# Float32 projections in a macaron block: Q, K, V and output products as one full-precision matmul each in place of three split ones

## Chip, cores and metric

The kernel runs on one core of a Trainium2 chip. The metric is the device time of one execution in microseconds (us). A page of the hardware profiler of one execution and the times of three runs are given.

## The reference, cut to what matters

Two batches of 2048 rows of 512 float32 numbers go through three residual steps: half a gated feed-forward block with 4-bit weights, then causal attention with 16 heads of 32, then the same feed-forward block again.

```python
x = L0_attn_X                                   # (2, 2048, 512) float32
x = x + 0.5 * ffn(layernorm(x))
x = x + attn(layernorm(x))
x = x + 0.5 * ffn(layernorm(x))

def attn(X):
    Xn = layernorm(X) * ln_g + ln_b
    Q, K, V = (split_heads(Xn @ W + b) for W, b in ((Wq, bq), (Wk, bk), (Wv, bv)))
    scores = Q @ K.T / sqrt(32)                  # causal mask, softmax, all float32
    AV = softmax(scores) @ V
    return AV @ Wo + bo
```

The change concerns the four products with `Wq`, `Wk`, `Wv` and `Wo`, each (4096 x 512) by (512 x 512), in float32.

## The kernel before, in words

**Order.** Five programs, one for each engine, walk the same plans and meet at semaphores: `tensor_program` (PE), `vector_program` (DVE), `scalar_program` (ACT), `gpsimd_program` (POOL), `sync_program` (SP, which issues all DMAs). Each runs the first feed-forward phase (`ffn_*`, f[0]), then for each batch b the projections (`qkv_*`), the attention (`att_*`) and the output projection (`out_*`), then the second feed-forward phase (f[1]). An engine takes its instructions strictly in the order written.

**Full-precision products out of split ones.** The array multiplies `float32r` operands at reduced precision in one pass. So a float32 operand x is kept as two float32r tiles: hi = x rounded (a copy by ACT or DVE), lo = x - hi (a subtraction by DVE). A product is then three matmuls into one PSUM bank: hi*hi, hi*lo, lo*hi. In this text a "product" is one 128-row by 128-column stationary tile against 128 x 512 moving numbers, and a "bank" is a sum of four products (KC = 4), thus 12 matmuls before.

**Projections** (`Qkv`, lines 828 to 1053). A row block tt holds 512 rows; a batch has four. `Qkv.order` (from line 866) writes the order of a batch: for tt = 0 the four `turn` events (transposes of the twice normed rows) with three `split` events among them, one for each weight matrix; then for each tt eight `features` banks (Q and K, transposed) and four `values` banks, each `values` followed by a `turn` of the next block. The last four `values` banks of a batch are spread over the start of the attention as 16 `value_part` events. A `turn` is four PE transposes into bank 0 or 1, one ACT `activation` with gain and bias into `xnt` (two small buffers, so it waits on `xl_made` of two turns before), then on DVE a copy to `xh` and a subtraction to `xl` (lines 990 to 1013). A `split` is an ACT copy of 128 x 2048 and a DVE subtraction of the same size. `qkv_project` (line 900) issues the three matmuls of each c and waits on `xl_made`. The layernorms of block tt+1 are 48 small DVE instructions, seven after each `features` bank; PE waits for them at the `turn`. The weights Wk and Wq are loaded at the "ahead" event of the last feed-forward block, Wv only after the last store of that phase (`ffn_sp`).

**Attention** (`Att`, lines 1056 to 1438). 160 steps a batch, in four head groups hg, each with query blocks qt = 0 to 3. Scores are f16 matmuls, ACT takes the exponential of each, and `weigh` and `total` are matmuls in true float32 whose stationary tile has 32 columns, four of them side by side in the array (128*32 in the profile). `max` units (96*128 matmuls and a DVE reduction) run ahead at a fixed pace. Into this order the plan puts four `wo_split` events from step (hg, qt, kt) = (2, 3, 0) and four `av_split` events from step (3, 2, 2): each is an ACT copy and a DVE subtraction of 128 x 512, for Wo and for the first quarter of the attention's result `avn`.

**Output projection** (`Out`, lines 1441 to 1580). 16 banks of four products. `out_act` and `out_dve` split the other three quarters of `avn` while PE works; DVE adds each bank to the residual, and does the norms of the next stage beside it. `out_sp` loads the residual rows, then the next weights: for b = 1 the pieces of the second feed-forward phase, of which those that lie where the output weights and split tiles are come late (four gate-and-up pieces, i = 4 to 7, after bank 15).

All matmuls are recorded at line 94 (`Eng.matmul`), transposes at 97, ACT at 100, DVE and POOL two-operand operations at 103, DMA issues at 133: these are helpers.

Of the kernel before, what the change touches and what calls it, by code (L numbers as in the profile page):

```python
# [3 lines left out]
F32 = mybir.dt.float32  # L4
# [19 lines left out]
C0 = 7936  # L24
# [743 lines left out]
def ffn_sp(e, p, f):  # L768
# [20 lines left out]
    for what, *at in f.plan:  # L789
# [31 lines left out]
    if f.ph == 0:  # L821
        e.wait_ge(*f.stored.at(NT - 1))
        p.qkv.weight_sp(e, 0, 2)
    else:
        e.wait_ge(*f.stored.at(NT - 1))


class Qkv:
    def __init__(self, p):
        self.p = p  # L830
        self.raw = [[p.at([128, KC, D], F32, o) for o in raw]
                    for raw in ((A0 + 24576, A0 + 32768, XR0), (C0 + 8192, C0, XR0))]
        o = QS0 + 32768
        self.wh = [p.at([128, KC, D], F32R, o + 16384 * i) for i in range(3)]
        self.wl = [p.at([128, KC, D], F32R, o + 16384 * i + 8192) for i in range(3)]
        self.xnt = [p.at([128, 512], F32, KP0 + 16384 + 2048 * i) for i in range(2)]
        self.q32 = [p.at([128, 512], F32, KP0 + 20480 + 2048 * i) for i in range(2)]
        xo = [KP0, o + 49152]
        self.xh = [p.at([128, KC, 512], F32R, xo[i]) for i in range(2)]
        self.xl = [p.at([128, KC, 512], F32R, xo[i] + 8192) for i in range(2)]  # L840
        self.x_in = p.sign("q_x_in", 16)
        self.w_in = [p.sign(f"q_w_in{n}", 16) for n in range(3)]
        names = ("normed", "turned", "xnt_made", "xh_made", "xl_made", "wh_made", "wl_made", "proj_done", "q_wide",
                 "q_hi", "q_lo", "v_made")
        (self.normed, self.turned, self.xnt_made, self.xh_made, self.xl_made, self.wh_made, self.wl_made,
         self.proj_done, self.q_wide, self.q_hi, self.q_lo, self.v_made) = (p.sign("q_" + x) for x in names)
# [11 lines left out]
    def weight_sp(self, e, b, n):  # L858
        w = self.p.a["L0_attn_" + ("Wq", "Wk", "Wv")[n]].rearrange("(c p) n -> p c n", p=128)
        e.dma_start(self.raw[b][n][:, :, :], w).then_inc(*self.w_in[n].up(b))  # L860
# [39 lines left out]
def qkv_project(e, p, b, tt, key, lh, ll, rh, rl):  # L900
# [16 lines left out]
def values_pe(e, p, b, tt, tb):  # L917
    q, i, c0 = p.qkv, tt % 2, slice(128 * tb, 128 * tb + 128)
    e.wait_ge(*q.wl_made.at((b, 2)))
    yield from qkv_project(e, p, b, tt, ("values", tt, tb), lambda c: q.xh[i][:, c, c0], lambda c: q.xl[i][:, c, c0],  # L920
                           lambda c: q.wh[2][:, c, :], lambda c: q.wl[2][:, c, :])


def qkv_pe(e, p, b):
    q = p.qkv
    for what, *at in q.order(b):
# [13 lines left out]
        elif what == "features":  # L940
# [7 lines left out]
            e.wait_ge(*q.wl_made.at((b, n)))  # L948
            for _ in qkv_project(e, p, b, tt, ("features", tt, f, n), lambda c: q.wh[n][:, c, fs],
                                 lambda c: q.wl[n][:, c, fs], lambda c: q.xh[i][:, c, :], lambda c: q.xl[i][:, c, :]):  # L950
                pass
# [5 lines left out]
def qkv_act(e, p, b):  # L957
    q = p.qkv
    for what, *at in q.order(b):
        if what == "turn":  # L960
            tt, c = at
            e.wait_ge(*q.turned.at((b, tt, c)))
            if tt or c >= 2:
                last = (b, tt, c - 2) if c >= 2 else (b, tt - 1, c + 2)
                e.wait_ge(*q.xl_made.at(last))
            elif b == 0:
                e.wait_ge(*p.f[0].w_out.at("all"))
            e.activation(q.xnt[c % 2][:, :], p.b[c % 2], ACT.Identity, scale=p.bias[:, 0, c:c + 1],
                         bias=p.bias[:, 1, c:c + 1]).then_inc(*q.xnt_made.up((b, tt, c)))
        elif what == "split":  # L970
            n = at[0]
            e.wait_ge(*q.w_in[n].at(b))
            if n == 2 and b:
                for s in p.out.stored[0:2]:
                    e.wait_ge(*s.at((0, 3)))
            if n == 0:
                e.wait_ge(*q.wl_made.at((b, 1)))
            e.activation(q.wh[n][:, :, :], q.raw[b][n][:, :, :], ACT.Copy).then_inc(*q.wh_made.up((b, n)))
# [11 lines left out]
def qkv_dve(e, p, b):  # L990
    q = p.qkv
    gens = {}
    for what, *at in q.order(b):
        if what == "turn":
            tt, c = at
            i = tt % 2
            e.wait_ge(*q.xnt_made.at((b, tt, c)))
            if c == 0 and tt >= 2:
                e.wait_ge(*q.proj_done.at((b, "values", tt - 2, 3)))
            elif c == 0 and tt == 1 and b:  # L1000
                for s in p.out.stored:
                    e.wait_ge(*s.at((0, 3)))
            elif c == 0 and tt == 0 and b == 0:
                e.wait_ge(*p.f[0].w_out.at("all"))
# [4 lines left out]
        elif what == "split":  # L1009
            n = at[0]  # L1010
            e.wait_ge(*q.wh_made.at((b, n)))
            e.tensor_tensor(q.wl[n][:, :, :], q.raw[b][n][:, :, :], q.wh[n][:, :, :], ALU.subtract).then_inc(
                *q.wl_made.up((b, n)))
        elif what == "norm":
# [41 lines left out]
class Att:  # L1056
# [68 lines left out]
    def order(self, b):  # L1125
# [34 lines left out]
        for n in range(N + 3):  # L1160
# [149 lines left out]
def att_act(e, p, b):  # L1310
# [6 lines left out]
    for what, *at in t.plan[b]:  # L1317
        if what == "rows":
# [4 lines left out]
            elif hg == 0:  # L1323
                e.wait_ge(*p.qkv.xl_made.at((b, 3, 3)))
# [24 lines left out]
        elif what == "wo_split":  # L1349
            out_wo_act(e, p, b, at[0])  # L1350
        elif what == "av_split":
            out_split_act(e, p, b, *at)


def att_dve(e, p, b):
    t, V = p.att, p.V
    for what, *at in t.plan[b]:
# [32 lines left out]
        elif what == "wo_split":  # L1390
            out_wo_dve(e, p, b, at[0])
        elif what == "av_split":
            out_split_dve(e, p, b, *at)
# [25 lines left out]
def att_sp(e, p, b):  # L1419
    t = p.att  # L1420
    for what, *at in t.plan[b]:
# [12 lines left out]
        elif what == "wo":  # L1434
            for j in range(4):
                e.wait_ge(*t.stacked[1][j].at((b, 3)))
            e.dma_start(p.out.wraw[:, :, :], p.a["L0_attn_Wo"].rearrange("(c p) n -> p c n", p=128)).then_inc(
# [3 lines left out]
class Out:  # L1441
    def __init__(self, p):
        self.p = p
        o = QS0 + 32768
        self.wraw = p.at([128, KC, D], F32, C0 + 8192)
        self.wh, self.wl = (p.at([128, KC, D], F32R, C0 + 16384 + 8192 * i) for i in range(2))
        self.ah = [p.at([128, KC, 512], F32R, x) for x in (KP0, o)]
        self.al = [p.at([128, KC, 512], F32R, x + 8192) for x in (KP0, o)]
# [232 lines left out]
```

## Time and profile before

| | |
|---|---|
| median of three runs | 2980.32 us (2968.59 to 2982.92) |
| time of the profiled execution | 2964.9 us |
| its span, first to last instruction | 2963.1 us |
| mean granted TensorE clock | 0.975 of full speed |
| PE / PE weight loads / DVE / ACT / POOL busy | 92% / 55% / 73% / 47% / 50% of the span |
| stages (us from the span's start) | feed-forward 0 to 720; projections 732 to 870 and 1530 to 1664; attention up to 1473 and 2268; output projections 1476 to 1523 and 2272 to 2318; feed-forward 2320 to 2963 |

How to read it: a busy engine is one with an instruction under way. A matmul's record is longer than the time after which the next one can start, so the pace of a stream is read from the distance of starts. "PEclk" is the granted clock of the array, 1.00 for 2.4 GHz and 0.50 for 1.2 GHz. A bracket at the end of a timeline row says how long the engine was idle before it and what ended that.

### The profile page before, as it was taken

What the parts mean: (1) busy time and instruction counts of PE and PEld (TensorE: products, weight loads), DVE (VectorE), ACT (ScalarE), POOL (GpSimd) and SP (SyncE); (2) the same over time, 40 slices, a digit from 0 to 9 for tenths busy, and PEclk for the clock granted to TensorE, in tenths of its full rate; (3) what the DMA queues carried; (4) which work ended last, traced back from release to release, by engine and by line L of the source; (5) the groups of instructions that cost most, each with busy time, mean ns of one, the idle gap of its engine ahead of it and who ended that gap; (6) DMA issues with size and microseconds to landing.
All of it is one profiled execution on the core that took longest, in us unless ns stands there. A gap on an engine that the chain in (4) does not pass through costs nothing.

```text
span 2963.1 us, 39754 instructions
## 1 busy us (share of the span) xinstructions
PE 2716.4 (92%) x14559; PEld 1623.7 (55%) x14559; DVE 2157.6 (73%) x3834; ACT 1381.1 (47%) x2667; POOL 1494.4 (50%) x1015
## 2 busy tenths in 40 slices
PE   6799999997998999988899899999988999999998
PEld 4677777775773333322277523332324777777776
DVE  8877777777758777777287587777763777777765
ACT  4444554544213555555522245555554354544554
POOL 5555555553222665555732145555557355555554
PEclk8999999998999999999999999999999999999999
DMA  2022201121022010200140300211003401111101
GB/s 58 15 88 75 113 33 35 43 81 62 29 50 54 5 45 5 59 5 2 37 150 29 89 16 5 45 30 35 4 3 141 172 15 43 43 43 43 43 29 43
DMA packets 75713, 142.12 MB, mean 48 GB/s; under 512 B 18783, under 2 KB 22394, under 8 KB 75390
## 3 DMA queue, kind: packets, MB, share of 16 engines
q1 hardware_dynamic: 75518, 139.58, 15.0%
q8 instruction: 115, 1.88, 0.3%
q14 instruction: 80, 0.66, 0.1%
HBM read 74.00 MB, written 37.22 MB: 38 GB/s over the span
## 4 chain that ended last, share of the span: by engine, by line
PE 55%; DVE 22%; ACT 9%; issue 6%; POOL 2%; SPq 1%; DMA 1%; POOLq 0%; ACTq 0%; DVEq 0%
PE pp L94 42%; PE ps L94 13%; DVE sb L109 9%; ACT sb L100 8%; DVE sb L115 3%; DVE sb L106 3%; DVE sb L103 2%; DVE sb L121 2%; POOL sb L103 2%; SPq L133 1%; DVE sb L118 1%; DVE sb L112 1%; DMA sb<-xa 1%; PE ps L97 0%; DVE sb L124 0%
## 5 line engine op out<-in xcount | busy, mean ns | idle before, releaser
L94 PE MATMUL pp<-sb,sb 128*128 128x512 f32 (+8 forms) x11154 | 2221.4, 435 | 130.3 <-ACT sb L100 33.9
L103 POOL TENSOR_TENSOR sb<-sb,sb 128x512 f32<-128x512 f32 (+6 forms) x998 | 1486.9, 1507 | 1453.4 <-ACT sb L100 594.1
L94 PEld LDWEIGHTS pp<-sb,sb 128*128 128x128 f32 (+3 forms) x11154 | 1196.3, 143 | 855.8 <-ACT sb L100 196.7
L100 ACT ACTIVATE sb<-pp 128x512 f32<-128x512 f32 (+4 forms) x1434 | 674.2, 548 | 546.7 <-PE pp L94 528.7
L94 PE MATMUL ps<-sb,sb 128*128 128x512 f32 (+5 forms) x2862 | 765.9, 362 | 72.3 <-DVE sb L109 25.1
L100 ACT ACTIVATE sb<-sb 128x512 f32<-128x512 f32 (+3 forms) x468 | 300.9, 649 | 680.2 <-DVE sb L109 559.5
L94 PEld LDWEIGHTS ps<-sb,sb 128*128 128x128 f32 (+3 forms) x2862 | 382.0, 148 | 413.7 <-DVE sb L115 197.8
L115 DVE TENSOR_REDUCE sb<-ps 128x1 f32<-128x512 f32 (+3 forms) x754 | 488.4, 670 | 156.4 <-PE ps L94 154.7
L109 DVE SCALAR_TENSOR_TENSOR sb<-ps,sb,sb 128x512 f32<-128x512 f32 x437 | 321.5, 745 | 139.1 <-PE ps L94 121.3
L109 DVE SCALAR_TENSOR_TENSOR sb<-pp,sb,sb 128x512 f32<-128x512 f32 x443 | 324.4, 743 | 119.6 <-PE pp L94 106.2
L115 DVE TENSOR_REDUCE sb<-pp 128x1 f32<-128x512 f32 (+2 forms) x366 | 243.0, 664 | 80.2 <-PE pp L94 79.5
L100 ACT ACTIVATE sb<-pp,sb 128x512 f32<-128x512 f32 x325 | 218.7, 678 | 135.7 <-PE pp L94 114.7
L100 ACT ACTIVATE sb<-ps,sb 128x512 f32<-128x512 f32 x299 | 198.1, 686 | 94.6 <-PE ps L97 90.2
L118 DVE RECIPROCAL sb<-pp 128x64 f32<-128x64 f32 x256 | 114.5, 508 | 99.0 <-PE pp L94 99.0
L103 DVE TENSOR_TENSOR sb<-sb,sb 128x512 fp32r<-128x512 f32 (+4 forms) x165 | 131.6, 822 | 8.8 <-ACT sb L100 6.5
L109 DVE SCALAR_TENSOR_TENSOR sb<-sb 128x4 f32<-128x4 f32 x288 | 106.2, 369 | 6.1
L106 DVE TENSOR_SCALAR sb<-sb 128x4 int32<-128x4 int32 (+2 forms) x233 | 91.7, 410 | 24.4 <-ACT sb L100 20.4
L103 DVE TENSOR_TENSOR sb<-pp,sb 128x512 f32<-128x512 f32 (+1 forms) x95 | 65.0, 688 | 52.4 <-PE pp L94 30.1
L112 DVE CAST sb<-sb 128x512 f16<-128x512 f32 (+2 forms) x128 | 58.6, 458 | 57.6 <-ACT sb L100 56.3
L100 ACT ACTIVATE sb<-ps 128x512 fp32r<-128x512 f32 (+1 forms) x73 | 43.0, 591 | 113.3 <-PE ps L94 73.5
L121 DVE BATCH_NORM_STATS2 sb<-sb 128x6 f32<-128x512 f32 x128 | 86.6, 677 | 11.6 <-DMA sb<-L_attn_X 6.5
L109 DVE SCALAR_TENSOR_TENSOR sb<-sb,sb,sb 128x512 f32<-128x512 f32 x64 | 79.5, 1282 | 0.5
(19 smaller groups left out, 360.9 us busy)
## 6 DMA issues: line engine op xcount, KB each, us to landing
sb<-sb SPq DMA_DIRECT2D x192, 128.0 KB, 2.4
sb<-L_attn_X SPq DMA_DIRECT2D x64, 256.0 KB, 4.0
sb<-xa SPq DMA_DIRECT2D x64, 256.0 KB, 5.3
sb<-xc SPq DMA_DIRECT2D x64, 256.0 KB, 4.3
xa<-sb SPq DMA_DIRECT2D x32, 256.0 KB, 2.0
xc<-sb SPq DMA_DIRECT2D x32, 256.0 KB, 3.7
out<-sb SPq DMA_DIRECT2D x32, 256.0 KB, 2.0
dg<-sb SPq DMA_DIRECT2D x11, 512.0 KB, 8.7
```

The source lines that it names most:

```text
L94: return self.e.matmul(*a, **k) if self.e else self
L100: return self.e.activation(*a, **k) if self.e else self
L103: return self.e.tensor_tensor(*a, **k) if self.e else self
L106: return self.e.tensor_scalar(*a, **k) if self.e else self
L109: return self.e.scalar_tensor_tensor(*a, **k) if self.e else self
L112: return self.e.tensor_copy(*a, **k) if self.e else self
L115: return self.e.reduce_max(*a, **k) if self.e else self
L118: return self.e.reciprocal(*a, **k) if self.e else self
L121: return self.e.bn_stats(*a, **k) if self.e else self
L133: return self.e.dma_start(*a, **k) if self.e else self
```

## The change

All tiles `wh`, `wl`, `xh`, `xl`, `ah`, `al` and what made them are gone. Weights are loaded straight into float32 tiles `w`; the turned rows go to a float32 `xnt` of a whole block, twice buffered; the output projection reads `avn` itself. Each product is one `matmul` with float32 operands.

```diff
+def product(e, out, left, right, start, stop):
+    return e.matmul(out, left, right, start=start, stop=stop)
...
     for c in range(KC):
-        e.wait_ge(*q.xl_made.at((b, tt, c)))
-        e.matmul(bank, lh(c), rh(c), start=c == 0, stop=False)
-        e.matmul(bank, lh(c), rl(c), start=False, stop=False)
-        k = e.matmul(bank, ll(c), rh(c), start=False, stop=c == KC - 1)
+        e.wait_ge(*q.xnt_made.at((b, tt, c)))
+        k = product(e, bank, left(c), right(c), c == 0, c == KC - 1)
```

The order of a batch loses its `split` events, and DVE its part of a `turn`; the wait of ACT is on the reader of the buffer two blocks before:

```diff
     def order(self, b):
-        yield "turn", 0, 0
-        yield "turn", 0, 1
-        yield "split", 1
-        yield "turn", 0, 2
-        yield "turn", 0, 3
-        yield "split", 0
-        yield "split", 2
+        for c in range(KC):
+            yield "turn", 0, c
         yield "load", 1
...
-            if tt or c >= 2:
-                last = (b, tt, c - 2) if c >= 2 else (b, tt - 1, c + 2)
-                e.wait_ge(*q.xl_made.at(last))
+            if tt >= 2:
+                e.wait_ge(*q.proj_done.at((b, "values", tt - 2, 3)))
+            elif tt == 1 and b:
+                for s in p.out.stored:
+                    e.wait_ge(*s.at((0, 3)))
...
-            e.tensor_copy(q.xh[i][:, c, :], q.xnt[c % 2][:, :]).then_inc(*q.xh_made.up((b, tt, c)))
-            e.wait_ge(*q.xh_made.now())
-            e.tensor_tensor(q.xl[i][:, c, :], q.xnt[c % 2][:, :], q.xh[i][:, c, :], ALU.subtract).then_inc(
-                *q.xl_made.up((b, tt, c)))
```

In the attention the eight split events of a batch go, in the output projection the splits of the other quarters:

```diff
-                if steps[n] == (2, 3, 0):
-                    parts += [("wo_split", c) for c in range(KC)]
-                if steps[n] == (3, 2, 2):
-                    parts += [("av_split", 0, c) for c in range(KC)]
...
+        e.wait_ge(*o.w_in.at(b))
         for c in range(KC):
-            e.wait_ge(*o.al_made.at((b, q, c)))
-            e.wait_ge(*o.wl_made.at((b, c)))
-            e.matmul(p.b[n % 8], o.ah[i][:, c, c0], o.wh[:, c, :], start=c == 0, stop=False)
-            e.matmul(p.b[n % 8], o.ah[i][:, c, c0], o.wl[:, c, :], start=False, stop=False)
-            k = e.matmul(p.b[n % 8], o.al[i][:, c, c0], o.wh[:, c, :], start=False, stop=c == KC - 1)
+            e.wait_ge(*t.normed.at((b, c, q)))
+            k = product(e, p.b[n % 8], p.avn[:, c, 128 * n:128 * n + 128], o.w[:, c, :], c == 0, c == KC - 1)
```

DMAs: Wv of the first batch is loaded with Wk and Wq in the last feed-forward block; the weights of the second batch no longer wait for a split; the pieces of the second feed-forward phase come in another order.

```diff
-            e.wait_ge(*f.gu_done.at((0, IC - 1, KC - 1, 1)))
-            for n in (1, 0):
+            e.wait_ge(*f.gu_done.at((NT - 2, IC - 1, KC - 1, 0)))
+            for n in (1, 0, 2):
                 q.weight_sp(e, 0, n)
...
-    first = [x for i in (0, 1, 2, 3, 4, 8, 9, 10) for x in ((i, 0), (i, 1)) if x not in ((4, 0), (8, 1))]
+    first = [x for i in range(IC) for x in ((i, 0), (i, 1)) if x not in ((2, 0), (3, 0))]
...
-            if n == 12:
-                e.wait_ge(*o.done.at((1, 11)))
-                for i in range(5, 9):
-                    load_piece_sp(e, p, f, i, 1)
...
-        for i in range(4, 8):
+        for i in range(2, 4):
             load_piece_sp(e, p, f, i, 0)
```

## Rows read from the trace of the kernel before

**Rows 1.** The page: span, busy time of each engine, chain that ended last.

```profile
span 2963.1 us, 39754 instructions
PE 2716.4 (92%) x14559; PEld 1623.7 (55%) x14559; DVE 2157.6 (73%) x3834; ACT 1381.1 (47%) x2667; POOL 1494.4 (50%) x1015
PE 55%; DVE 22%; ACT 9%; issue 6%; POOL 2%; SPq 1%; DMA 1%; POOLq 0%; ACTq 0%; DVEq 0%
```

**Rows 2.** Groups by shape on PE: shapes, count, busy us, mean ns of one.

```profile
L94 PE MATMUL pp<-sb,sb 128*128 128x512 f32 x4960 | 1287.8, 400 | 58.7 <-DVE sb L109 29.4 <-DVE sb L103 24.4 <-POOL sb L103 1.7
...
L94 PE MATMUL pp<-sb,sb 128*32 128x512 f32 x2816 | 376.1, 610 | 9.1 <-DVE sb L118 9.1
...
L94 PE MATMUL pp<-sb,sb 128*32 128x128 f32 x256 | 13.6, 284 | 0.0
```

**Rows 3.** Timeline, attention: eight records of float32, then the next start.

```profile
947.65 1.06 PE L94 MATMUL pp<-sb,sb 128*32 128x512 f32 x8
948.65 0.39 PE L94 MATMUL ps<-sb,sb 96*128 96x512 f16 x1
```

**Rows 4.** Timeline, second batch's projections: two banks of features drained by ACT.

```profile
1613.02 0.69 ACT L100 ACTIVATE sb<-pp,sb 128x512 f32<-128x512 f32 x1 [2.03 <-PE pp L94]
...
1615.74 0.69 ACT L100 ACTIVATE sb<-pp,sb 128x512 f32<-128x512 f32 x1 [2.03 <-PE pp L94]
```

**Rows 5.** Timeline, first batch: transposes, first matmul, ACT's first weight split, attention's first matmul.

```profile
723.14 1.78 PE L97 MATMUL ps<-sb,sb 128*128 128x128 f32 x8 [3.53 <-ACT sb L100]
723.65 1.90 ACT L100 ACTIVATE sb<-sb 128x2048 fp32r<-128x2048 f32 x1
...
732.01 27.15 PE L94 MATMUL pp<-sb,sb 128*128 128x512 f32 x108 [7.08 <-DVE sb L103]
...
870.31 0.52 PE L94 MATMUL ps<-sb,sb 96*128 96x128 f16 x6
```

**Rows 6.** Timeline of PE, second batch: last transposes, first matmul, attention's first two.

```profile
1524.96 1.32 PE L97 MATMUL ps<-sb,sb 128*128 128x128 f32 x8 [0.43 <-ACT sb L100]
...
1529.76 27.67 PE L94 MATMUL pp<-sb,sb 128*128 128x512 f32 x108 [3.47 <-DVE sb L103]
...
1664.27 0.52 PE L94 MATMUL ps<-sb,sb 96*128 96x128 f16 x6
1668.03 0.29 PE L94 MATMUL ps<-sb,sb 96*128 96x128 f16 x2 [3.24 <-DMA sb<-sb]
```

**Rows 7.** Timeline of PE at a block's end: transposes, then two banks of values.

```profile
797.76 1.61 PE L97 MATMUL ps<-sb,sb 128*128 128x128 f32 x4 [1.22 <-DVE sb L106]
799.12 3.00 PE L94 MATMUL pp<-sb,sb 128*128 128x512 f32 x12
...
802.31 3.02 PE L94 MATMUL pp<-sb,sb 128*128 128x512 f32 x12
```

**Rows 8.** Stretches: length, busy of PE, PEld, DVE, ACT, POOL, then PEclk.

```profile
732.00:737.00 5.00, 4.99 (x12) 3.95 (x13) 4.17 (x5) 3.25 (x2) 0.00 (x0) 0.50 0.98 355
...
1102.24:1203.38 101.14, 97.55 (x690) 32.42 (x689) 79.02 (x139) 55.85 (x118) 59.61 (x31) 1.00 0.08 17
1241.34:1351.44 110.10, 100.91 (x687) 32.95 (x686) 85.86 (x141) 58.00 (x122) 60.15 (x31) 0.95 0.01 4
1402.00:1408.00 6.00, 6.00 (x27) 1.47 (x26) 4.06 (x8) 2.28 (x4) 1.07 (x1) 0.65 0.00 0
```

**Rows 9.** Timeline at the split of the first quarter of the attention's result.

```profile
1393.16 6.81 POOL L103 TENSOR_TENSOR sb<-sb,sb 128x512 f32<-128x512 f32 x3 [0.75 <-DVE sb L118]
...
1393.83 7.29 DVE L103 TENSOR_TENSOR sb<-sb,sb 128x512 fp32r<-128x512 f32 x4 [0.75 <-ACT sb L100]
...
1401.78 0.61 PE L94 MATMUL pp<-sb,sb 96*128 96x512 f16 x1 [4.01 <-DVE sb L115]
```

**Rows 10.** Timeline of PE, first output projection: its first and last groups of matmuls.

```profile
1476.34 8.05 PE L94 MATMUL ps<-sb,sb 128*128 128x512 f32 x24 [3.87 <-DVE sb L118]
...
1505.98 16.48 PE L94 MATMUL pp<-sb,sb 128*128 128x512 f32 x72
```

**Rows 11.** DMA issues: count, KB each, median us from issue to landing.

```profile
sb<-dg SPq DMA_DIRECT2D x11, 512.0 KB, 7.5
```

More of the change, by code:

```diff
@@ L830, in __init__ @@
         self.p = p
-        self.raw = [[p.at([128, KC, D], F32, o) for o in raw]
-                    for raw in ((A0 + 24576, A0 + 32768, XR0), (C0 + 8192, C0, XR0))]
         o = QS0 + 32768
-        self.wh = [p.at([128, KC, D], F32R, o + 16384 * i) for i in range(3)]
-        self.wl = [p.at([128, KC, D], F32R, o + 16384 * i + 8192) for i in range(3)]
-        self.xnt = [p.at([128, 512], F32, KP0 + 16384 + 2048 * i) for i in range(2)]
+        self.w = [p.at([128, KC, D], F32, o + 8192 * i) for i in (1, 0, 2)]
         self.q32 = [p.at([128, 512], F32, KP0 + 20480 + 2048 * i) for i in range(2)]
-        xo = [KP0, o + 49152]
-        self.xh = [p.at([128, KC, 512], F32R, xo[i]) for i in range(2)]
-        self.xl = [p.at([128, KC, 512], F32R, xo[i] + 8192) for i in range(2)]
+        self.xnt = [p.at([128, KC, 512], F32, x) for x in (KP0, o + 49152)]
         self.x_in = p.sign("q_x_in", 16)
         self.w_in = [p.sign(f"q_w_in{n}", 16) for n in range(3)]
[L843 to L846, printed above, removed]
+        names = ("normed", "turned", "xnt_made", "proj_done", "q_wide", "q_hi", "q_lo", "v_made")
+        (self.normed, self.turned, self.xnt_made, self.proj_done, self.q_wide, self.q_hi, self.q_lo, self.v_made) = (
+            p.sign("q_" + x) for x in names)
         self.src = p.xa.rearrange("(b n t p) d -> b n t p d", b=B, t=4, p=128)
@@ L918, in values_pe @@
     q, i, c0 = p.qkv, tt % 2, slice(128 * tb, 128 * tb + 128)
-    e.wait_ge(*q.wl_made.at((b, 2)))
-    yield from qkv_project(e, p, b, tt, ("values", tt, tb), lambda c: q.xh[i][:, c, c0], lambda c: q.xl[i][:, c, c0],
-                           lambda c: q.wh[2][:, c, :], lambda c: q.wl[2][:, c, :])
+    e.wait_ge(*q.w_in[2].at(b))
+    yield from qkv_project(e, p, b, tt, ("values", tt, tb), lambda c: q.xnt[i][:, c, c0], lambda c: q.w[2][:, c, :])
 def qkv_pe(e, p, b):
@@ L947, in qkv_pe @@
                     e.wait_ge(*p.out.y_made.at((0, 15)))
-            e.wait_ge(*q.wl_made.at((b, n)))
-            for _ in qkv_project(e, p, b, tt, ("features", tt, f, n), lambda c: q.wh[n][:, c, fs],
-                                 lambda c: q.wl[n][:, c, fs], lambda c: q.xh[i][:, c, :], lambda c: q.xl[i][:, c, :]):
+            e.wait_ge(*q.w_in[n].at(b))
+            for _ in qkv_project(e, p, b, tt, ("features", tt, f, n), lambda c: q.w[n][:, c, fs],
+                                 lambda c: q.xnt[i][:, c, :]):
                 pass
@@ L962, in qkv_act @@
             e.wait_ge(*q.turned.at((b, tt, c)))
-            if tt or c >= 2:
-                last = (b, tt, c - 2) if c >= 2 else (b, tt - 1, c + 2)
-                e.wait_ge(*q.xl_made.at(last))
+            if tt >= 2:
[3 more added lines that the diff above has]
+                    e.wait_ge(*s.at((0, 3)))
             elif b == 0:
                 e.wait_ge(*p.f[0].w_out.at("all"))
-            e.activation(q.xnt[c % 2][:, :], p.b[c % 2], ACT.Identity, scale=p.bias[:, 0, c:c + 1],
+            e.activation(q.xnt[tt % 2][:, c, :], p.b[c % 2], ACT.Identity, scale=p.bias[:, 0, c:c + 1],
                          bias=p.bias[:, 1, c:c + 1]).then_inc(*q.xnt_made.up((b, tt, c)))
[L970 to L978, printed above, removed]
         elif what == "features":
@@ L993, in qkv_dve @@
     for what, *at in q.order(b):
[L994 to L1004, printed above, removed]
-            e.tensor_copy(q.xh[i][:, c, :], q.xnt[c % 2][:, :]).then_inc(*q.xh_made.up((b, tt, c)))
-            e.wait_ge(*q.xh_made.now())
-            e.tensor_tensor(q.xl[i][:, c, :], q.xnt[c % 2][:, :], q.xh[i][:, c, :], ALU.subtract).then_inc(
-                *q.xl_made.up((b, tt, c)))
[L1009 to L1014, printed above, removed]
+        if what == "norm":
             if at[0] not in gens:
@@ L1436, in att_sp @@
                 e.wait_ge(*t.stacked[1][j].at((b, 3)))
-            e.dma_start(p.out.wraw[:, :, :], p.a["L0_attn_Wo"].rearrange("(c p) n -> p c n", p=128)).then_inc(
+            e.dma_start(p.out.w[:, :, :], p.a["L0_attn_Wo"].rearrange("(c p) n -> p c n", p=128)).then_inc(
                 *p.out.w_in.up(b))
@@ L1444, in __init__ @@
         o = QS0 + 32768
[L1445 to L1448, printed above, removed]
+        self.w = p.at([128, KC, D], F32, C0 + 8192)
         self.xr = [[p.at([128, 512], F32, (o + 32768 if i < 12 or b == 0 else XR0 - 24576) + 2048 * i)
@@ L1453, in __init__ @@
         self.stored = [p.sign(f"o_stored{q}", 16) for q in range(4)]
-        (self.wh_made, self.wl_made, self.ah_made, self.al_made, self.biased, self.done, self.y_made) = (
-            p.sign("o_" + x) for x in ("wh_made", "wl_made", "ah_made", "al_made", "biased", "done", "y_made"))
+        self.biased, self.done, self.y_made = (p.sign("o_" + x) for x in ("biased", "done", "y_made"))
         self.src = p.xa.rearrange("(b n t p) d -> b n t p d", b=B, t=4, p=128)
@@ L1527, in out_dve @@
         q, tb = divmod(n, 4)
-        if tb == 0 and q < 3:
-            for c in range(KC):
-                out_split_dve(e, p, b, q + 1, c)
         x = o.xr[b][n][:, :]
```

50 lines of the change are left out of this document (3 added, 47 removed).

## The prediction

> **What bounds the kernel now.** I read the page first: PE is busy for 92% of the span and carries 55% of the chain that ended last, DVE 22% [rows 1]. So the array is the bound, but a fifth of the chain is DVE's. The groups by shape then show two kinds of float32 matmul: the split ones with a full stationary tile, 400 ns each, and those of the attention, which the program writes with true float32 operands and 32 stationary columns, 610 ns each at 512 columns [rows 2]. The timeline of the projections gives the pace of the first kind, that of the attention the pace of the second. Last I looked for stretches in which PE waits for the splits, because only there does the removal of DVE and ACT work gain time.
>
> **What one product costs.** *Before.* In an undisturbed stretch ACT drains one bank of 12 matmuls every 1615.74 - 1613.02 = 2.72 us and had waited 2.03 us for PE each time [rows 4]: 0.2267 us a matmul, 0.680 us a product of three.
>
> *After.* No row shows a float32 matmul with a full stationary tile. The nearest are the 32-column ones. By the program there are 1408 of them at 512 columns in both batches (224 `weigh` and 128 `total` steps of four), and the trace has 2816 records [rows 2]: the hardware runs each as two. From 128 to 512 columns such a record grows from 284 to 610 ns [rows 2], 0.85 ns a column, where a column at 2.4 GHz takes 0.42: each record streams its columns twice, so a float32 matmul is four passes, 4 x 512 / 2.4 GHz = 0.853 us. Four tiles side by side, eight records, take 948.65 - 947.65 = 1.00 us from start to next start [rows 3]. These are the bounds: 0.853 with nothing between records, 1.00 with the overhead of eight. A product on the whole array has two records. A single matmul now costs 0.2267 - 0.2133 = 0.013 us above its columns [rows 4]; two of these on 0.853 give **0.88 us**, which I take, since the operand shape and the 128-column weight load beside it are those of that row. Weight loads have 0.43 us of matmul to hide behind, instead of 0.23. So a product costs 0.20 us more, a bank 3.52 in place of 2.72, and with 512 products the bare sum would be +102 us.
>
> The Trainium skill, FP8 and Floating Point Precision, TensorE Precision Notes, says that true float32 takes four passes through the array, high and low parts each with each. The trace agrees on the count of four. Were each of the four a matmul at today's pace [rows 4], a product would take 0.907 us and the sum below would be 14 us higher.
>
> **Projections, tt = 0 to 2 and the features of tt = 3** (176 products, 44 banks, 12 turns a batch). A turn before a bank of values costs 802.31 - 799.12 - 2.72 = 0.47 us of PE [rows 7]. Undisturbed, the stretch would take 44 x 2.72 + 12 x 0.47 = 125.3 us; it took 870.31 - 732.01 = 138.3 [rows 5] and 1664.27 - 1529.76 = 134.5 [rows 6]. Of the excess some 2.5 us is the slow clock at the start (0.50 for 5 us, [rows 8]), which I leave in. The rest is PE waiting at the three block ends for DVE's second norm: 1.22 us idle and then transposes paced by DVE [rows 7]. DVE needs some 27 us from the last transposes of a block (load, 48 norm steps, 8 casts), and PE offers nine banks: 24.5 us now, 31.7 after. So DVE drops behind PE, and the waits go, also because its copies, subtractions and weight splits go. After: 44 x 3.52 + 5.6 + 2.5 = 163.0. That is +24.7 and +28.5: **+53.2**. If the block-end waits stayed, 17 us more.
>
> **Starts of the two projections.** The last transposes end at about 724.7 and 1526.1; the first matmul starts at 732.01 and 1529.76, held by DVE's splits [rows 5, 6]. ACT puts a weight split of 1.90 us among the turns [rows 5]. After, a matmul needs only ACT's turned rows, 0.8 us behind the transposes, and the fourth of them is needed three products later. **-7.3 and -3.7**. The residual additions of DVE at the end of the feed-forward phase still stand, but nobody on PE waits for them. Wv comes with Wk and Wq during the last feed-forward block; its one issue moves past SP's load of residual rows there, which is needed a block later.
>
> **Last values, 16 products beside the first max units.** +3.2 us a batch. Against it PE waits for the stacking DMAs: 3.24 us idle in the second batch [rows 6], 2.2 in the first. They start when the second bank of tt = 3 is drained, and six more banks follow, 21.1 us in place of 16.3, so they land in time. With the slow clock after that wait about 1 us each more: **-1** in all; if the waits stay, +6.
>
> **Attention.** Eight ACT copies (0.63 us) and eight DVE subtractions go in each batch. Busy time alone would be nothing, but here they stall PE. At the second cluster DVE takes 7.29 us for four subtractions of 0.69, beside 6.81 us of POOL [rows 9]: two reads from SBUF on DVE wait until POOL is done. The max reductions queue behind them, PE stands for 4.01 us [rows 9], and its clock falls to a mean of 0.65 for 6 us [rows 8]: 4 + 2 us, and ACT's copies before it, 6.5 in all. For the first cluster I compare the same 28 steps of two head groups: 101.14 us in the second, 110.10 in the third, with 690 and 687 matmul records and PE idle for 3.6 and 9.2 us [rows 8]. I take 8 of the 9. Two batches: **-29**. Bounds: 0, if other DVE work slides into the same place, and -34. What is next late there is ACT's exponentials and POOL's sums; the rows before and after the clusters already run at their pace.
>
> **Output projections.** PE starts after the last reciprocal in both kernels. Now 1505.98 + 16.48 - 1476.34 = 46.1 us [rows 10] for 64 products: 43.5 and 2.6 of slow clock. After: 56.3 + 2.5 = 58.8. DVE's and ACT's splits were beside PE, so nothing returns. **+12.7** a batch, +25.4.
>
> **Second feed-forward phase.** Its gate-and-up pieces 2 and 3 now come last, after bank 15. They need about 7.5 us each [rows 11], and PE reaches step 2 some 14 us after the phase begins. I cost this at nothing, hidden by steps 0 and 1; without that cover 5 us.
>
> **Sum:** 53.2 - 11.0 - 1 - 29 + 25.4 = +37.6, say **+37**. On the profiled execution of 2964.9 us that is 3002. The three runs lie 4 to 18 us above it, their median 15; I add 8: **3010 us**. A measurement of this kernel can tell about 0.5%, 15 us, from no change.
>
> **Rivals.**
> - *The forecast*, 2988 to 3035: product of 0.853 to 0.90, most waits gone. 0.62.
> - *Attention gives nothing back.* The clusters were only where a general shortage showed, and the max units now crowd elsewhere. For it: DVE is 73% busy. Against: the clean head group with as many records has 9 us less. 3010 + 29 = 3039. 0.12.
> - *A product costs 1.00 us*, weight loads or the change of record not hidden. For it: the eight records took that [rows 3]. Against: they were eight, not two. +61: 3071. 0.10.
> - *Four full passes of 0.2267 us.* 0.907 a product, as two matmuls' overhead in each record would make it: 3024. 0.08. That is what the page named above would give with today's pace.
> - *Other side: a cheap product.* With a whole stationary tile one of the two records streams its columns once, so a product is three passes as now, 0.68 us; the price is -102, the time 2908. It decides below 0.81 us a product (0.88 - 37/512). For it: no row shows a whole tile in float32. Against: the slope in rows 2 is twice that of one pass. 0.08.
>
> **How the numbers follow.** Slower by over 0.5%: 0.48 of the forecast's 0.62 and the three dear rivals, 0.30, together 0.78. Within 0.5%: 0.14, the forecast's low end (0.853 a product takes 14 us off, a warm clock at the second start 3, a little more won in the attention). Faster: 0.08, the cheap product. The range of 2985 to 3050 leaves out the 1.00 us product and the cheap one, 0.18.
>
> **What would show it.** PE records at the projections: 1024 of the new kind, mean near 0.61 us, none of the 1536. ACT's distance between banks: 3.52 us; 2.7 would prove the cheap product, 4.0 the dear one. First matmul near 724.7. No idle time of PE before the transposes of tt = 1 to 3. The third head group as long as the second, near 101 us, with PEclk 1.00. Output stage 59 us. PE's busy share near 94%, DVE's near 68%. If PE waits for `dg` in the last phase, that step was wrong.

## The result, and the profile after

Four runs of the changed kernel lie between 3009.49 and 3010.45 us, median **3010.39**. Beside them the kernel before took 2974.45 us (median of four, 2967.64 to 2982.92). The ratio is **1.0119, interval 1.0086 to 1.0152**: slower by 1.2%, and the range of the prediction holds it. A later and larger sample of the kernel before, 13 runs, has its median at 2978.88, so the change is worth about +31.5 us from median to median. Of all executions used below, one of the kernel with float32 in the output projection alone (3572.91 us, mean granted clock 0.698) was in a slow state and is left out.

The page of the changed kernel, its span, busy times and chain:

```profile
span 3008.7 us, 38513 instructions
PE 2790.5 (93%) x14047; PEld 1532.8 (51%) x14047; DVE 2063.9 (69%) x3724; ACT 1350.3 (45%) x2621; POOL 1486.5 (49%) x1015
PE 64%; DVE 16%; ACT 8%; issue 5%; POOL 2%; DMA 0%; SPq 0%; POOLq 0%; ACTq 0%; DVEq 0%
```

Against [rows 1] PE is busy for 74 us more and DVE for 94 us less. The chain that ended last has moved with them: 64% PE and 16% DVE, where it had been 55% and 22%. The waits behind DVE went, and PE's work grew by more.

The timeline of PE in the first batch: the projections' start, one block of features, two banks of values, and attention's first matmul.

```profile
737.48 1.97 PE L97 MATMUL ps<-sb,sb 128*128 128x128 f32 x8 [3.53 <-ACT sb L100]
739.24 21.23 PE L94 MATMUL pp<-sb,sb 128*128 128x512 f32 x45
...
783.95 31.07 PE L94 MATMUL pp<-sb,sb 128*128 128x512 f32 x72
814.86 0.60 PE L97 MATMUL ps<-sb,sb 128*128 128x128 f32 x4
815.29 3.60 PE L94 MATMUL pp<-sb,sb 128*128 128x512 f32 x8
818.73 0.60 PE L97 MATMUL ps<-sb,sb 128*128 128x128 f32 x4
...
898.19 0.63 PE L94 MATMUL ps<-sb,sb 96*128 96x128 f16 x8
```

Three things are read here. First the price: eight banks of features are 32 products, and the values bank behind them, merged into the same row, is four more. 72 records for 36 products make two a product, and start to next start is 814.86 - 783.95 = 30.91 us, so **0.8586 us a product**, at a granted clock of 1.00 (the window below, columns as in [rows 8]). Second, the block end has no bracket: where [rows 7] had PE idle for 1.22 us, it turns and goes on. Third, the first matmul starts as the last group of transposes ends (739.24, beside 737.48 + 1.97), where PE had stood idle for 7.08 us [rows 5].

```profile
783.95:814.86 30.91, 30.91 (x75) 13.64 (x74) 21.95 (x57) 6.27 (x9) 9.47 (x8) 1.00 0.10 34
```

ACT's drains of three banks of features give the same price a second way, 3.435 us a bank, where [rows 4] had 2.72.

```profile
787.59 0.69 ACT L100 ACTIVATE sb<-pp,sb 128x512 f32<-128x512 f32 x1 [2.66 <-PE pp L94]
791.02 0.69 ACT L100 ACTIVATE sb<-pp,sb 128x512 f32<-128x512 f32 x1 [2.75 <-PE pp L94]
794.46 0.69 ACT L100 ACTIVATE sb<-pp,sb 128x512 f32<-128x512 f32 x1 [2.75 <-PE pp L94]
```

The output projection of the first batch:

```profile
1491.76 9.76 PE L94 MATMUL ps<-sb,sb 128*128 128x512 f32 x16 [3.87 <-DVE sb L118]
1501.36 20.76 PE L94 MATMUL pp<-sb,sb 128*128 128x512 f32 x48
1521.96 7.03 PE L94 MATMUL ps<-sb,sb 128*128 128x512 f32 x16
1528.82 20.76 PE L94 MATMUL pp<-sb,sb 128*128 128x512 f32 x48
...
1553.06 7.46 PE L94 MATMUL pp<-sb,sb 128*128 128x512 f32 x17
```

It is 128 records for 64 products. The first 16 take 2.7 us longer than the 16 at 1521.96: the array comes out of 3.87 us of waiting, and its mean granted clock is 0.72 over these 9.6 us and 1.00 at 1521.96. The stage lasts 1549.58 - 1491.76 = 57.8 us, where [rows 10] give 46.1.

The two stretches of the attention that held the split events, and the clean head group before them (stretches as in [rows 8]: length, busy of PE, PEld, DVE, ACT, POOL, PEclk):

```profile
1128.37:1229.53 101.16, 97.56 (x691) 32.43 (x689) 79.11 (x139) 55.85 (x118) 59.64 (x31) 1.00 0.08 19
1267.50:1373.40 105.90, 99.46 (x694) 33.08 (x693) 82.90 (x140) 56.22 (x118) 59.15 (x31) 0.98 0.02 5
1411.32:1448.47 37.15, 33.84 (x237) 10.18 (x236) 16.39 (x33) 23.31 (x50) 23.98 (x14) 1.00 0.01 4
```

The second head group is unchanged. The third takes 105.9 us (104.7 in the second batch), down from 110.1 (110.3) but not to the 101 of the second, and its clock is 0.98, not 1.00. The stretch of the second cluster takes 37.15; of the kernel before it is, in the same view:

```profile
1389.06:1433.07 44.01, 36.69 (x241) 10.74 (x240) 25.57 (x40) 25.46 (x54) 24.89 (x14) 0.92 0.01 3
```

### The profile page after: what moved, and what is told of

The parts are those of the page before. It is cut to its first block, busy times and chain, and to the rows that moved or that the text cites. A ratio compares the mean times of both kernels' runs of the same rounds, so it can differ in the third digit from the quotient of the medians.

```text
span 3008.7 us, 38513 instructions
## 1 busy us (share of the span) xinstructions
PE 2790.5 (93%) x14047; PEld 1532.8 (51%) x14047; DVE 2063.9 (69%) x3724; ACT 1350.3 (45%) x2621; POOL 1486.5 (49%) x1015
## 4 chain that ended last, share of the span: by engine, by line
PE 64%; DVE 16%; ACT 8%; issue 5%; POOL 2%; DMA 0%; SPq 0%; POOLq 0%; ACTq 0%; DVEq 0%
PE pp L94 50%; PE ps L94 13%; DVE sb L109 8%; ACT sb L100 8%; DVE sb L115 3%; POOL sb L103 2%; DVE sb L106 1%; DVE sb L118 1%; DVE sb L103 1%; DVE sb L121 1%; PE ps L97 1%; DVE sb L112 1%; DMA sb<-sb 0%; SPq L133 0%; DVE sb L124 0%
## 5 line engine op out<-in xcount | busy, mean ns | idle before, releaser
L94 PE MATMUL pp<-sb,sb 128*128 128x512 f32 (+8 forms) x10674 | 2290.1, 453 | 109.1 <-DVE sb L109 32.4
L94 PEld LDWEIGHTS pp<-sb,sb 128*128 128x128 f32 (+4 forms) x10674 | 1106.7, 141 | 973.4 <-issue 364.0
L94 PE MATMUL ps<-sb,sb 128*128 128x512 f32 (+6 forms) x2830 | 770.7, 366 | 73.8 <-DVE sb L109 30.1
L100 ACT ACTIVATE sb<-sb 128x512 fp32r<-128x512 f32 (+4 forms) x422 | 266.4, 632 | 634.9 <-DVE sb L109 567.8
L106 DVE TENSOR_SCALAR sb<-sb 128x4 int32<-128x4 int32 (+2 forms) x233 | 105.2, 467 | 24.4 <-ACT sb L100 20.5
L112 DVE CAST sb<-sb 128x512 f16<-128x512 f32 (+1 forms) x96 | 47.2, 491 | 82.6 <-ACT sb L100 81.5
L106 DVE TENSOR_SCALAR sb<-sb,sb,sb 128x512 f32<-128x512 f32 x128 | 79.4, 650 | 0.5
## 6 DMA issues: line engine op xcount, KB each, us to landing
sb<-sb SPq DMA_DIRECT2D x192, 128.0 KB, 2.4
```

The costliest lines, as they stand in the source:

```text
L94: return self.e.matmul(*a, **k) if self.e else self
L100: return self.e.activation(*a, **k) if self.e else self
L106: return self.e.tensor_scalar(*a, **k) if self.e else self
L112: return self.e.tensor_copy(*a, **k) if self.e else self
```

## Where 45.6 us between the two profiled spans came from

Stage boundaries are starts of instructions that both programs have (the first projection matmul, the reciprocals of the attention, and so on). The stretches that are not listed agree within 0.1 us in all; with them the differences add up to that of the spans, 3008.7 - 2963.1, but for rounding. The first boundary is DVE's first instruction of the second row block's layernorm scaling.

| stage | before | after | difference | forecast |
|---|---|---|---|---|
| first row block of the first feed-forward phase | 128.1 | 141.1 | +13.1 | 0 |
| rest of that phase | 590.5 | 591.8 | +1.3 | 0 |
| last transposes to first projection matmul (batch 0, 1) | 13.4, 6.3 | 6.3, 2.7 | -10.7 | -11.0 |
| projections | 138.3, 134.5 | 159.0, 157.2 | +43.3 | +53.2 |
| attention to its first reciprocal | 56.5, 57.6 | 54.8, 55.6 | -3.8 | -1 |
| stretch of the Wo splits | 52.1, 52.2 | 47.5, 46.2 | -10.6 | -16 |
| the two stretches behind it | 95.6, 95.7 | 96.3, 96.4 | +1.4 | 0 |
| stretch of the first-quarter splits | 44.0, 44.0 | 37.2, 37.2 | -13.7 | -13 |
| output projections | 47.1, 46.2 | 58.6, 58.0 | +23.3 | +25.4 |
| second feed-forward phase | 645.2 | 647.2 | +2.0 | 0 |

The stretch of the Wo splits and the two behind it are best read together, -9.2: the reciprocal that parts them is an instruction of DVE, and in the first batch PE's part before it is 323 matmul records in the kernel before and 304 in the changed one.

The lines that the change touches add up to +31.2 (forecast +37); 14.3 us lie in the first phase, of whose code the change touches only when three loads are issued near its end. The +31.2 agrees with the +31.5 between the medians, and the extra 14 is the subject of two experiments below.

## Experiments

**The splits out of the attention's third head group, nothing else.** The kernel before, with both clusters put off to the last steps of the attention:

```diff
-                if steps[n] == (2, 3, 0):
+                if steps[n] == (3, 3, 3):
                     parts += [("wo_split", c) for c in range(KC)]
-                if steps[n] == (3, 2, 2):
+                if steps[n] == (3, 3, 8):
                     parts += [("av_split", 0, c) for c in range(KC)]
```

> The kernel before, with the eight split events of a batch moved in the attention's plan: wo_split from step (2, 3, 0) to (3, 3, 3), av_split from (3, 2, 2) to (3, 3, 8), where DVE has no max reductions left. Nothing else changes, products stay three matmuls. Theory (splits in the attention stall PE because DVE waits for POOL and the max units queue behind DVE; worth 14.5 us a batch): 25 us below the kernel before (29 less some 2 us a batch for ACT copies in the last steps), the third head group 101 to 103 us long in place of 110. Rival (a general shortage of DVE or ACT, the clusters only show it): within 5 us of the kernel before.

Measured: median 2956.51 us, ratio 0.993 (0.9906 to 0.9954), and 17.1 us less span than the kernel before, where 25 had been expected; and the third head group, expected at 101 to 103 us, takes 106. The windows of the third head group and of the two stretches behind it:

```profile
1239.45:1345.70 106.25, 99.62 (x695) 33.16 (x694) 83.02 (x140) 56.19 (x118) 59.23 (x31) 0.98 0.02 5
1383.60:1420.74 37.14, 33.83 (x237) 10.18 (x236) 16.38 (x32) 23.31 (x50) 23.96 (x14) 1.00 0.01 3
1420.74:1462.60 41.86, 36.24 (x256) 9.53 (x254) 15.32 (x17) 31.53 (x67) 35.40 (x17) 1.00 0.00 1
```

With three split matmuls everywhere the first two stretches are those of the changed kernel, 106.2 for 105.9 and 37.14 for 37.15. So what the attention got back is what the splits cost in their place, and the rival "attention gives nothing" falls. Not all of it can be had this way: the third stretch, where the splits now stand, takes 41.9 us for 39.5 (43.5 in the second batch). That the cleared third head group stays near 106 us and not 101 shows here too: those 5 us were not the cost of the splits.

**Which half of a split costs.** ACT's copies stay where they were, DVE's subtractions alone are put off:

```diff
                 if steps[n] == (2, 3, 0):
-                    parts += [("wo_split", c) for c in range(KC)]
+                    parts += [("wo_copy", c) for c in range(KC)]
                 if steps[n] == (3, 2, 2):
-                    parts += [("av_split", 0, c) for c in range(KC)]
+                    parts += [("av_copy", 0, c) for c in range(KC)]
+                if steps[n] == (3, 3, 3):
+                    parts += [("wo_split", c) for c in range(KC)]
...
```

> The kernel before with the eight split events of a batch pulled apart: ACT's copies stay at steps (2, 3, 0) and (3, 2, 2), only DVE's subtractions move to (3, 3, 3) and (3, 3, 8). Theory (DVE's subtractions, held by POOL, are what stalls PE in the attention): as the run with both moved, the second-to-third query blocks of head group three 105 to 107 us and the next head group's 37 to 38 us from (3, 1) to (3, 2), less than 1 us worse each. Rival (ACT's copies in the chain of exponentials cost the time): 109 us or more, and 42 or more.

Measured: median 2954.47 us, ratio 0.9922 (0.9894 to 0.9951). The same two stretches, expected at 105 to 107 and 37 to 38 us:

```profile
1245.37:1349.30 103.93, 97.88 (x687) 32.39 (x686) 79.47 (x136) 57.89 (x122) 59.17 (x31) 0.98 0.02 4
1386.98:1424.80 37.82, 34.51 (x242) 10.37 (x240) 18.36 (x35) 25.25 (x54) 23.99 (x14) 1.00 0.01 3
```

PE's timeline at the copies of the first quarter, which begins like that of the kernel before record by record:

```profile
1393.17 0.38 PE L94 MATMUL ps<-sb,sb 96*128 96x384 f16 x2
...
1394.35 1.71 PE L94 MATMUL pp<-sb,sb 128*128 128x512 f16 x10 [0.36 <-ACT sb L100]
1395.89 0.38 PE L94 MATMUL ps<-sb,sb 96*128 96x512 f16 x1
1396.11 0.60 PE L94 MATMUL pp<-sb,sb 128*128 128x512 f16 x2
```

It goes on at 1395.89, where the kernel before then stood for 4.01 us behind the max reductions [rows 9]. ACT's four copies cost the stretch 0.7 us (37.82 for 37.15), DVE's four subtractions 6.2 (44.01 for 37.82): the prediction's reading of rows 9, DVE held while POOL works and the reductions queued behind it, stands, and the rival that ACT's copies cost the time falls (109 and 42 us or more). Why the third head group is another 2.3 us shorter here than with all splits late stays open.

**The output projection alone in float32.** The kernel before with the three split products kept for Q, K and V; `Wo` and `avn` read as they are, and the eight split events of the attention gone with them.

```diff
-            e.matmul(p.b[n % 8], o.ah[i][:, c, c0], o.wh[:, c, :], start=c == 0, stop=False)
-            e.matmul(p.b[n % 8], o.ah[i][:, c, c0], o.wl[:, c, :], start=False, stop=False)
-            k = e.matmul(p.b[n % 8], o.al[i][:, c, c0], o.wh[:, c, :], start=False, stop=c == KC - 1)
+            k = product(e, p.b[n % 8], p.avn[:, c, 128 * n:128 * n + 128], o.w[:, c, :], c == 0, c == KC - 1)
```

> The kernel before with the change made in the output projection alone (float32 Wo and attention result, no splits in the attention or beside the output matmuls, the new order of the late weight pieces); Q, K and V keep their three split matmuls. Theory: attention -29, output 128 products x (0.858 - 0.680) = +23, so 6 us below the kernel before, and the attention's intervals equal those of the changed kernel within 1 us. Rival (attention gives nothing back): +23.

Measured: median 2979.98 us of nine runs (2966.83 to 2983.93), ratio 0.9996 (0.9981 to 1.001): no change, where 6 us less had been expected. The profiled span shows the two halves apart. Attention 595.5 and 595.8 us for 606.0 and 607.4, together -22.1 (29 expected); output 58.7 and 57.7 us for 47.1 and 46.2, together +23.1; second feed-forward phase +1.9, from the other order of the late weight pieces, which this kernel shares with the changed one. A quarter of the products thus about pays for itself through what surrounds it. The other three quarters, in the projections, have no such refund.

**A cheap product in the same program.** The changed kernel, each product as three bf16 matmuls on the high halves alone; the low halves are left out of the sum, so this measures only time.

```diff
-    return e.matmul(out, left, right, start=start, stop=stop)
+    left, right = left.bitcast(BF16)[:, 1::2], right.bitcast(BF16)[:, 1::2]
+    e.matmul(out, left, right, start=start, stop=False)
+    e.matmul(out, left, right, start=False, stop=False)
+    return e.matmul(out, left, right, start=False, stop=stop)
```

> The changed kernel, but each product is three one-pass bf16 matmuls on the high halves of the same float32 tiles in place of one float32 matmul; the low halves are left out of the computation and each product is summed three times. All of the change but the four passes is kept. Theory (the change is a dearer product of 0.858 us and cheaper everything else): a product costs 0.65 us, 512 x 0.21 = 108 us less than the changed kernel, up to 17 of it given back by block-end waits on DVE's norms, so 2902 to 2919. Rival (PE is not the bound in the projections, the waits are general): above 2940.

Measured: median 2942.08 us, ratio 0.9874 (0.9844 to 0.9903). The expectation missed: 2902 to 2919 had been given, and the time lies just inside the rival's range (above 2940). PE's timeline over the first two block ends:

```profile
725.06 25.40 PE L94 MATMUL pp<-sb,sb 128*128 128x512 bf16 x108
755.93 1.84 PE L97 MATMUL ps<-sb,sb 128*128 128x128 f32 x4 [5.47 <-DVE sb L106]
...
768.71 24.46 PE L94 MATMUL pp<-sb,sb 128*128 128x512 bf16 x108
794.64 1.70 PE L97 MATMUL ps<-sb,sb 128*128 128x128 f32 x4 [1.47 <-DVE sb L106]
```

A product is 0.68 us here (24.46 us for 108 matmuls, three to a product), and PE waits 5.47 and 1.47 us at the block ends for DVE's second norm, though DVE has no split left to make. Over the whole stretch these waits are 8.3 and 4.0 us in the two batches; in the kernel before they were 3.8 and 1.6, in the changed kernel PE has no wait above 0.15 us there. The projections take 141.3 and 135.5 us, no less than before the change, while the starts stay as short as after it (6.2 and 2.7). So two parts of the mechanism come apart. The short starts are due to the missing splits. The missing waits at block ends are due to the dear product: 31 us of matmuls a block cover DVE's norms, 24.5 do not. Over 512 products the cheaper one saves 0.18 us each, 91 us; the span without its first block is shorter by 2936.2 - 128.2 against 3008.7 - 141.1, 59.6 us. The other third is given back, 23.5 us of it in the projections and 8 in the last values behind them, where PE's waits for the stacking DMAs are back (2.2 and 3.0 us). So the theory had the product too cheap (0.65) and the waits too short (up to 17 us). The rival's reading does not follow from its number: in the changed kernel PE works through the projections without a wait, and only with a cheap product is DVE the next bound there.

**The first row block, 1: move one decode slice.** In the changed kernel:

```diff
-                        yield "decode", i + 3, 5 if c < 3 else 99
+                        yield "decode", i + 3, 4 if c < 3 else 99
```

> The changed kernel with one edit in the first feed-forward block, which the change does not touch: DVE's 13 decode instructions for a later weight tile are spread 4, 4, 5 over three places in place of 5, 5, 3. In the profile of the changed kernel that block ends 13 us later than in the kernel before. Theory A (it is the phase in which DVE's decode instructions and POOL's scaling meet, and code elsewhere only shifts it): the block's length moves by 5 us or more either way, and the rest of the kernel keeps its length within 2 us. Theory B (something of the change itself, as its loads, makes the block longer): the block stays at 141 us to its first norm, within 2 us.

Measured: median 3005.05 us, ratio 1.0095 (1.0078 to 1.0112). The first row block takes 136.4 us for 141.1, every later stage as in the changed kernel within 2 us. Theory A had asked for a move of 5 us or more, theory B for one of at most 2; the 4.7 us meet neither. Since the block's length differs by up to 13 us between kernels in which nobody edited it (last section), this run by itself does not show that the place of DVE's decoding moves it, and this slicing does not bring back the 128.1.

**The first row block, 2: fewer POOL instructions beside DVE.** In the changed kernel, two of the three scalings of the decoded weights go to ACT:

```diff
+def scale_act(e, p, f, m):
+    i, part = divmod(m, 3)
+    if part == 2 or m >= 3 * IC:
+        return
...
+    for g in range(4):
+        v = p.vv[:, :, o + 32 * g:o + 32 * g + 32].bitcast(F16).rearrange("p b q -> p q b")
+        k = e.activation(p.w32[m % 2][:, g, :].rearrange("p (q b) -> p q b", b=4), v, ACT.Copy, scale=16384.0)
...
-            e.wait_ge(*f.scaled.at(at[0]))
+            e.wait_ge(*(f.scaled if part == 2 else f.scaled_act).at(at[0]))
```

> The changed kernel with one edit in the first feed-forward block: of the 33 scalings of decoded weights (float16 to float32, POOL, 1.35 us each) the 22 with a constant scale go to ACT, four instructions each; the 11 others stay on POOL. Theory A (the block's length is set by DVE's two-byte decode instructions standing still while POOL has an instruction of its own under way; POOL now has less of them): the first norm of the second block at 120 to 130 us in place of 141, DVE's 88 decode TENSOR_SCALARs below 45 us in place of 50, the four executions below 3000 us, the rest as in the changed kernel within 2 us. Theory B (the block is set by something else, and ACT now becomes late for PE): 141 us or more.

Measured: median 2984.61 us, ratio 1.0032 (1.0017 to 1.0048); the first block 119.6 us (120 to 130 expected), the rest of the phase 2.3 us less, every stage behind it as in the changed kernel within 2 us. The groups by shape on DVE in the first 150 us:

```profile
L106 DVE TENSOR_SCALAR sb<-sb 128x384 uint16<-128x384 uint16 x88 | 31.0, 394 | 1.2
```

Against 610 ns in the changed kernel (fence in the last section) one such instruction now takes 394. With less of POOL beside DVE, 26 us of the changed kernel's time goes, nearly as much as the change had cost.

**Both cures, three split products kept.** The kernel before with the splits late and the scalings on ACT.

> The kernel before (three split matmuls a product) with the late splits of the first run and the scalings of the fifth, to see whether it beats both kernels. If the two gains add: 17 to 22 us from the attention and 5 to 15 from the first block, 2940 to 2952 against a kernel before at 2979. If the first block does not gain: 2957.

Measured: median **2939.6 us** of six runs (2936.8 to 2943.54), ratio **0.9876 (0.9856 to 0.9896)**. Its page:

```profile
span 2938.1 us, 39820 instructions
PE 2706.1 (92%) x14559; PEld 1621.6 (55%) x14559; DVE 2142.0 (73%) x3834; ACT 1407.6 (48%) x2755; POOL 1467.8 (50%) x993
```

Both gains add: the median is 0.4 us below the 2940 to 2952 expected for that, and the first block takes 117.6 us. It is 71 us below the changed kernel and 38 below the kernel before (2977.22, median of 17 beside it), and every engine's busy share is that of the kernel before within a point. The products are the same as before; only the splits and the scalings stand in better places.

## Why the prediction was right, and which of its terms were not

**One product, 0.88 forecast, 0.8586 measured.** The four passes were right, in two records a product, 598 ns each on average (0.61 us forecast). The failed part is the overhead: it took twice the 0.013 us that a single matmul shows above its columns, once for each of two records. Measured is 0.8586 - 0.8533 = 0.005 us for both. The lower of the two bounds was the near one. The rival of four passes at today's pace, 0.907 us, is excluded, and so are the cheap product and the one of 1.00 us. The Trainium skill, FP8 and Floating Point Precision, TensorE Precision Notes, gives four passes for true float32; the trace agrees, since 0.8586 is four times 512 columns at 2.4 GHz and 0.6% more.

**Projections, +53.2 forecast, +43.3.** The forecast's own formula with the measured bank, 44 x 3.435 + 5.6 + 2.5 = 159.2 us, meets the 159.0 of the first batch. In the second the first 5 us ran at the slow clock before and do not now, so its 2.5 us falls away: 156.7 for 157.2. The windows of these 5 us, first of the kernel before, then of the changed one:

```profile
1529.76:1534.76 5.00, 5.00 (x12) 3.94 (x13) 4.93 (x6) 3.71 (x2) 0.00 (x0) 0.50 0.18 63
```

```profile
1553.06:1558.06 5.00, 5.00 (x14) 2.28 (x13) 0.43 (x1) 1.66 (x3) 0.14 (x1) 1.00 0.62 206
```

The forecast had this warm clock in its low end and not in its sum. That the waits at block ends go held. The cheap product shows why: the length of PE's own work hides them, and not DVE's relief, which the forecast named beside it ("also because its copies, subtractions and weight splits go").

**Starts, -7.3 and -3.7 forecast, -7.1 and -3.6.** Held.

**Last values and the stacking DMAs, -1 forecast, -3.8.** Right in sign, and the waits named, 2.2 and 3.2 us, are gone from the trace. With the cheap product they are back (2.2 and 3.0), so it is the dear product that hides them. The rest of the size was not tried.

**Attention, -29 forecast, -24 for the stretches of the two clusters, -23 with those between them.** The second cluster was read from its own stall and came out to half a microsecond (-6.5 a batch forecast, -6.9 measured). The first was read from a comparison of two head groups, 110.1 against 101.1 us, "I take 8 of the 9". That step failed. Over the same 28 steps the gain is 4.2 us, and 5.6 in the second batch. Cleared of the subtractions, the third head group takes 103.9, 105.9 and 106.2 us in three kernels. It has 3 to 5 us of its own that the second has not, and the difference of two stretches had been booked whole on the one suspect. The rows spoke against it: PE's idle time of 9.2 and 3.6 us in the two head groups differs by 5.6 us only, not by 9, and no stall of the size of rows 9 was shown for the third.

**Output projections, +12.7 each forecast, +11.5 and +11.8.** The product's 0.02 us, taken 64 times, is 1.4 us and about what was too much.

**Second feed-forward phase, 0 forecast, +2.0.** The waits for `dg` that the forecast named as a sign of error did not come: in both kernels PE's longest wait there is 2.3 us, for DVE. The 2.0 us stand in the output-only kernel too (+1.9) and not in the one with late splits (+0.4), so they go with the changed order of the pieces or of the tiles in memory; which of the two was not tried.

**The sum.** The forecast was too dear by 12 us in projections and output (mostly the product) and by 3 in the last values, too cheap by 8 in the attention behind them and the last phase: +37.6 came out as +31.2. The 8 us for the way from profile to median had been read off three runs. The 13 later runs have their median 14 us above the profiled execution, one of the quick ones: 2964.9 + 31 + 14 is the measured 3010. So one term was six too large and the other six too small, and that the forecast met the median to a microsecond is luck.

## What to carry to other kernels

A true float32 matmul on the whole array costs its four passes and next to nothing more, so against three split passes it costs a quarter more PE time (0.8586 for 0.680 us), and it pays only where making the splits stalls PE: here for the output projection, at even, and not for the projections. Before buying such relief with a dearer instruction, move the helpers: DVE subtractions put where no reduction queues behind them gave 22 us for two changed lines. And a stall is sized by its own rows; the difference between two stretches has in it all else in which they differ.

## What the runs showed that was not expected

The first row block, whose code is the same in both kernels, takes 128.1 us in one profile and 141.1 in the other; over all profiles here with that code it is 128.0 to 141.1: late splits 128.0, cheap product 128.2, output only 130.3, subtractions late 131.9. The groups by shape on DVE in the first 175 us, of the kernel before:

```profile
L106 DVE TENSOR_SCALAR sb<-sb 128x384 uint16<-128x384 uint16 x88 | 37.4, 467 | 1.1
```

and of the changed kernel:

```profile
L106 DVE TENSOR_SCALAR sb<-sb 128x384 uint16<-128x384 uint16 x88 | 50.2, 610 | 1.1
```

The same 88 instructions take 12.8 us longer. Not all of it is loss: DVE's 44 instructions of two uint16 operands take 14.4 us in place of 21.0. What reaches PE is in its waits over the block, of the kernel before (us in total, times, longest):

```profile
PE pp L94 <- DVE sb L109: 13.0, 4, 5.1
...
PE ps L94 <- DVE sb L109: 9.1, 4, 3.0
```

and of the changed kernel:

```profile
PE pp L94 <- DVE sb L109: 15.7, 4, 4.5
PE ps L94 <- DVE sb L109: 15.3, 4, 4.9
```

That is 8.9 us more of standing behind DVE in this kind of wait alone. The timeline shows who starts first. Kernel before:

```profile
43.08 1.97 DVE L106 TENSOR_SCALAR sb<-sb 128x384 uint16<-128x384 uint16 x4
43.63 5.22 POOL L103 TENSOR_TENSOR sb<-sb,sb 128x512 f32<-128x512 f32 x4 [0.61 <-ACT sb L100]
...
47.76 2.08 PE L94 MATMUL ps<-sb,sb 128*128 128x512 f32 x4 [2.52 <-DVE sb L109]
```

Changed kernel, the same place:

```profile
43.81 5.12 POOL L103 TENSOR_TENSOR sb<-sb,sb 128x512 f32<-128x512 f32 x4 [0.34 <-ACT sb L100]
...
44.19 4.86 DVE L106 TENSOR_SCALAR sb<-sb 128x384 uint16<-128x384 uint16 x4
...
50.69 2.08 PE L94 MATMUL ps<-sb,sb 128*128 128x512 f32 x4 [4.94 <-DVE sb L109]
51.15 0.41 DVE L106 TENSOR_SCALAR sb<-sb 128x384 uint16<-128x384 uint16 x2
```

Alone, two of these DVE instructions take 0.41 us. Where POOL's stream of four has begun 0.4 us before them, four take 4.86 us, about one to each of POOL's; where DVE begins first, the four take 1.97: three of them 0.71, and the fourth, which starts 0.08 us behind POOL's first, 1.34. PE waits 4.94 us in the one case and 2.52 in the other. The Trainium skill, SBUF — State Buffer, section "SBUF: two separate sides", says that DVE and GpSimd share a pair of ports as an exclusive lock, and that whichever of the two starts second is blocked for the other's whole instruction, when DVE runs in a two-port performance mode or reads two inputs from SBUF beside a GpSimd instruction that reads SBUF. The trace agrees in the blocking, with these numbers. The decode instructions have one tensor input, so it would be the first of the two cases; no run here shows the mode. What sets the phase at 43 us was not found. The programs differ only much later. The cheap-product kernel has the loads and the memory layout of the changed kernel and still takes 128.2 us, so it is neither of these; it may be the placement of code or the arrival of the first loads in time, and that stays open. That it is this block which spreads the runs of the kernel before (2960.98 to 2981.3 us in 17) was only argued: each kernel has one profile.
